# The last three pairs of a normalised matrix transposed by DMA in a fused graph layer on one Trainium2 core

## The reference, cut to what matters

```python
h = jnp.maximum(_layernorm(x, axis=-1), 0.0)            # "h0" below
type_sum = adj @ h                                      # the aggregate
attn_a = sigmoid(concat([type_sum, h], 1) @ Wa.T + ba)  # attn_b the same with Wb, bb
hw = h @ W_sa                                           # "mv" below, once scaled
s_left, s_right = hw @ a_sa[0, :256], hw @ a_sa[0, 256:]
scores = s_left[:, None] + s_right[None, :]
e = where(adj != 0, exp(-leaky_relu(scores, 0.01)), 0)
x_a = (e / (sum(e, 1) + 1e-5)) @ hw
x_b = adj @ (h @ W_gcnb) + b_gcnb                       # computed as (adj @ h) @ W_gcnb
out = x + sigmoid(attn_a * x_a + attn_b * x_b)
```

## Time and profile before

| | us |
|---|---|
| median of 3 runs (lowest, highest) | 179.05 (178.74, 179.24) |
| the profiled execution | 178.25 |
| its span in the trace | 176.4 |
| PE busy in the span | 171.6 |
| DVE busy | 147.0 |
| ACT busy | 115.4 |
| POOL busy | 18.6 |

### The profile page before, as it was taken

One profiled execution on the slowest core, in us unless ns is written; L12 is line 12 of the kernel. 1 busy time (PEld: TensorE's weight loads), 2 busy tenths in 40 slices (PEclk: granted clock), 3 DMA queues, 4 the chain that ended last, 5 costly groups with the idle time before them and its releaser, 6 DMA issues.

```text
span 176.4 us, 3397 instructions
## 1 busy us (share of the span) xinstructions
PE 171.6 (97%) x1324; PEld 125.8 (71%) x1324; DVE 147.0 (83%) x309; ACT 115.4 (65%) x169; POOL 18.6 (11%) x42
## 2 busy tenths in 40 slices
PE   7999999999999999999999999999999999999992
PEld 2556776654444468888844488888888888888892
DVE  3799997648999999799999922999999999976551
ACT  3679899642899988748494640675875884863310
POOL 4745436030000200000000000000000000000000
PEclk9999999999999999999999999999999999999999
DMA  5999996999991598000001100000010010011101
GB/s 129 288 260 260 224 181 116 202 206 211 298 423 43 82 214 180 0 4 2 0 4 59 59 0 4 0 0 0 4 59 0 6 59 0 4 61 59 60 33 30
DMA packets 5520, 16.87 MB, mean 96 GB/s; under 512 B 625, under 2 KB 1409, under 8 KB 4737
## 3 DMA queue, kind: packets, MB, share of 16 engines
q0 software_dynamic: 1584, 8.39, 24.6%
q1 hardware_dynamic: 3920, 8.27, 13.2%
HBM read 22.94 MB, written 2.11 MB: 142 GB/s over the span
## 4 chain that ended last, share of the span: by engine, by line
PE 94%; DMA 3%; DVE 1%; SPq 1%; issue 0%; ACT 0%; DVEq 0%
PE ps L773 31%; PE ps L815 16%; PE ps L816 16%; PE ps L814 16%; PE ps L751 6%; PE ps L807 6%; DMA wa_sb<-in_w_wide 3%; PE ps L745 2%; SPq L234 1%; PE ps L877 0%; DVE wa_hi L507 0%; DVE logit L724 0%; DVE e_lo L526 0%; ACT logit L411 0%; DVE res L631 0%
## 5 line engine op out<-in xcount | busy, mean ns | idle before, releaser
L814 PE MATMUL ps<-mv_lo,e_hi 128*128 128x257 f16 (+2 forms) x272 | 71.0, 267 | 0.0
L816 PE MATMUL ps<-mv_hi,e_lo 128*128 128x257 f16 (+2 forms) x272 | 70.8, 266 | 0.0
L815 PE MATMUL ps<-mv_hi,e_hi 128*128 128x257 f16 (+2 forms) x272 | 70.8, 266 | 0.0
L377 ACT ACTIVATE z<-z,log_e 128x1024 f32<-128x1024 f32 x32 | 36.7, 1146 | 29.1 <-DVE z L568 29.1
L568 DVE SCALAR_TENSOR_TENSOR z<-sl_row,exs,far 128x512 f32<-128x512 f32 x64 | 45.0, 743 | 0.0
L576 DVE TENSOR_TENSOR e_lo<-z,e_hi 128x1024 f16<-128x1024 f32 x32 | 38.9, 1216 | 1.2 <-ACT e_hi L387 1.2
L773 PE MATMUL ps<-adj,nat_lo 128*128 128x512 f16 x128 | 36.8, 379 | 0.0
L773 PE MATMUL ps<-adj,nat_hi 128*128 128x512 f16 x128 | 36.7, 379 | 0.0
L387 ACT ACTIVATE e_hi<-z 128x1024 f16<-128x1024 f32 x32 | 33.3, 1041 | 0.0
L815 PEld LDWEIGHTS ps<-mv_hi,e_hi 128*128 128x128 f16 x272 | 26.5, 98 | 3.2
L814 PEld LDWEIGHTS ps<-mv_lo,e_hi 128*128 128x128 f16 x272 | 26.4, 97 | 3.3
(11 more groups left out here) (69 smaller groups left out, 164.8 us busy)
## 6 DMA issues: line engine op xcount, KB each, us to landing
adj<-in_adj_t POOLq DMA_DIRECT2D x6, 1024.0 KB, 10.4
x_sb<-in_x SPq DMA_DIRECT2D x6, 512.0 KB, 8.9
out<-res SPq DMA_DIRECT2D x7, 256.0 KB, 2.0
adj<-in_adj_t POOLq DMA_DIRECT2D x3, 512.0 KB, 7.5
x_sb<-in_x SPq DMA_DIRECT2D x3, 256.0 KB, 4.8
sl_row<-sl_line SPq DMA_DIRECT2D x1, 768.0 KB, 9.7
adj<-in_adj_t POOLq DMA_DIRECT2D x2, 256.0 KB, 5.9
wa_sb<-in_w_wide SPq DMA_DIRECT2D x1, 258.0 KB, 4.5
```

Source lines behind the costliest of these rows:

```text
L377: act.activation(z[:, n % ZRING, :, :], z[:, n % ZRING, :, :], ACT.Exp, bias=log_e[:, 0:1], scale=SLOPE - 1.0).then_inc(exp_done, 1)
L814: pe.matmul(ps[:, bank, cols], e_hi[:, s, i1], mv_lo[:, j, cols], start=(j == 0), stop=False)
L815: pe.matmul(ps[:, bank, cols], e_hi[:, s, i1], mv_hi[:, j, cols], start=False, stop=False)
L816: return pe.matmul(ps[:, bank, cols], e_lo[:, s, i1], mv_hi[:, j, cols], start=False, stop=(j == NT - 1))
```

## The change

- PE transposes only units 0 to 5 (tiles 0 to 9, `NTURN` = 6). For pairs 5, 6 and 7 SP issues six DMA transposes (`turn_by_dma`), `nat_hi` and `nat_lo` of a pair each, straight into `h0t_hi` and `h0t_lo`; the layout of these becomes tile by tile. ACT and DVE no longer copy these three units out of PSUM.
- The wide products of pairs 5, 6, 7 (`wide(6)` to `wide(8)`) stand within the aggregate of chunk 1, after its tiles 7, 11 and 15. What follows from them on ACT (`mv_highs`) and DVE (`narrow_results`, `mv_lows`) stands in the loop over n, at n = 2 to 7.
- The row of s_left is in two halves of 8 tiles. `sl_lines(0)` stands at `wide(5)`, one unit later; `sl_lines(1)` after four tiles of the aggregate of chunk 2, on ACT at n = 8. `sl_spread(0)` stands on SP behind four of the six transposes, and now covers chunks 0 and 1.
- POOL asks for adj piece 5 one unit earlier, and waits for all six transposes before piece 7. SP asks for x again only when piece 7 has landed; the additions of 0.5 to it move from n = 2, 3, 4, 6 to 8, 9, 11, 12.

```diff
-SL_PARTS = ((0, 4), (4, 16))
-SL_UNIT = 4
+SL_PARTS = ((0, 8), (8, 16))
+SL_UNIT = 5
+LATE = 3
+ONTIME = NPAIR - LATE
+NTURN = NU - LATE
+WIDE_BANKS = (6, 2, 6, 2, 6, 2, 0, 2)
...
+            def turn_by_dma(p):
+                ts = slice(2 * p, 2 * p + 2)
+                for have, nat, h0t in ((nat_high, nat_hi, h0t_hi), (nat_ready, nat_lo, h0t_lo)):
+                    sp.wait_ge(have, p + 1)
+                    sp.dma_start(h0t[:, ts, :, :].rearrange("p t k n -> p (t k) n"),
+                                 nat[:, ts, :].rearrange("p t d -> p (t d)"),
+                                 transpose=True).then_inc(h0t_landed[p - ONTIME], 16)
+
+            sp.wait_ge(adj_landed[piece_of(0, NT - 1)], 16)
+            turn_by_dma(ONTIME)
             sl_store(0)
+            turn_by_dma(ONTIME + 1)
             sl_spread(0)
-            sl_store(1)
-            sp.wait_ge(turned, NU)
+            for p in range(ONTIME + 2, NPAIR):
+                turn_by_dma(p)
+            sp.wait_ge(adj_landed[piece_of(2, 0)], 16)
+            sp.wait_ge(turned, NTURN)
...
+            sl_store(1)
             sl_spread(1)
...
+            for p in range(ONTIME, NPAIR):
+                pool.wait_ge(h0t_landed[p - ONTIME], 32)
             load_adj(7)
...
-                    dve.wait_ge(sl_ready[min(c, 1)], 16)
+                    dve.wait_ge(sl_ready[c // 2], 16)
...
+                if n == 2:
+                    narrow_results(5)
+                if n == 3:
+                    mv_lows(5)
+                if n == 4:
+                    narrow_results(6)
+                if n == 5:
+                    mv_lows(6)
+                if n == 6:
+                    narrow_results(7)
                 if n == 7:
+                    mv_lows(7)
+                if n == 8:
                     agg_lows(1)
...
-            b_products(1, 0, 4)
-            pe.wait_ge(h0t_ready, NU)
+            b_products(1, 0, 8)
+            wide(6)
+            b_products(1, 8, 12)
+            pe.wait_ge(h0t_ready, NTURN)
+            wide(7)
+            b_products(1, 12, 16)
+            wide(8)
+            b_products(2, 0, 4)
             sl_lines(1)
-            b_products(1, 4, 16)
-            b_products(2, 0, 16)
+            b_products(2, 4, 16)
```

More of the change, by code:

```diff
@@ L136, in build @@
         part_b = sb("part_b", [P, 2, D], F32)
-        sl_turn = [part_b[0:hi - lo, h, 0:P] for h, (lo, hi) in enumerate(SL_PARTS)]
+        sl_turn = [c_sb[0:hi - lo, C_WT + h * P:C_WT + (h + 1) * P] for h, (lo, hi) in enumerate(SL_PARTS)]
         gated_b = sb("gated_b", [P, 2, 2, D], F32)
@@ L172, in build @@
         h0t_ready = sem("h0t_ready")
+        h0t_landed = [sem(f"h0t_landed{p}") for p in range(ONTIME, NPAIR)]
         wide_product = sem("wide_product")
@@ L310, in _ @@
             norms(5)
+            load_adj(5)
             norms(6)
-            load_adj(5)
             norms(7)
@@ L344, in h0t_highs @@
                 act.wait_ge(turned, u + 1)
-                act.activation(h0t_cols(h0t_hi, u), turn_bank(u), ACT.Copy).then_inc(h0t_high, 1)
+                act.activation(h0t_tiles(h0t_hi, u), turn_bank(u), ACT.Copy).then_inc(h0t_high, 1)
             def nat_highs(p):
@@ L431, in _ @@
                     nat_highs(p + 2)
-                mv_highs(p)
-            act.activation(factor_l[:, :], exs[:, :, SL], ACT.Exp, scale=SLOPE).then_inc(factors_done, 1)
+                if p < ONTIME - 1:
+                    mv_highs(p)
+            mv_highs(ONTIME - 1)
             agg_highs(0)
-            sl_lines(1)
             act.wait_ge(wg_landed, 16)
@@ L442, in _ @@
                     act_high(n - 1)
-                if n in (2, 3, 4):
-                    half_added(n - 2)
+                if n == 2:
+                    mv_highs(5)
+                if n == 4:
+                    mv_highs(6)
                 if n == 6:
+                    mv_highs(7)
+                    act.activation(factor_l[:, :], exs[:, :, SL], ACT.Exp, scale=SLOPE).then_inc(factors_done, 1)
+                if n == 7:
                     agg_highs(1)
-                    half_added(3)
+                if n == 8:
+                    sl_lines(1)
+                if n in (8, 9, 11, 12):
+                    half_added((8, 9, 11, 12).index(n))
                 if n == 10:
@@ L566, in dve_z @@
                 dve.wait_ge(far_ready, n + 1)
+                if ONTIME <= n < NPAIR:
+                    dve.wait_ge(exs_ready, n + 1)
                 for u in range(2):
@@ L651, in _ @@
             mv_lows(0)
-            for p in range(1, NPAIR):
-                if p + 1 < NPAIR:
-                    nat_lows(p + 1)
+            for p in range(1, ONTIME - 1):
+                nat_lows(p + 1)
                 if p > 1:
                     mv_lows(p - 1)
-                if p + 4 < NU:
-                    moments(p + 4)
+                moments(p + 4)
                 narrow_results(p)
-                if p + 1 < NPAIR:
-                    h0t_lows(p + 2)
-            mv_lows(NPAIR - 1)
+                h0t_lows(p + 2)
+            moments(NU - 1)
+            nat_lows(ONTIME)
+            mv_lows(ONTIME - 2)
+            narrow_results(ONTIME - 1)
+            for p in range(ONTIME + 1, NPAIR):
+                nat_lows(p)
+            mv_lows(ONTIME - 1)
             agg_lows(0)
@@ L755, in wide @@
             def wide(u):
-                pe.wait_ge(h0t_ready, u + 1)
+                if u < NTURN:
+                    pe.wait_ge(h0t_ready, u + 1)
+                else:
+                    pe.wait_ge(h0t_landed[u - NTURN], 32)
                 if u == 1:
```

34 lines of the change are left out of this document (18 added, 16 removed).

## The result

| | median, us | of runs | profiled execution | span | granted clock in it |
|---|---|---|---|---|---|
| before | 179.15 | 6 (178.43 to 179.63) | 178.25 | 176.4 | 1.00 |
| changed | 189.18 | 6 (186.22 to 192.42) | 186.22 | 184.4 | 0.991 |

The changed kernel is slower. The forecast was 183.2.

A forecast was written before the change was run, and what follows sets the result against it. PE, busy 97% of the span, was taken to bound the kernel. A 5.5 us wait for exs (57.8 against 52.3) less 1.3 dropped gave +4.2 on 179.05: 183.2 us, range 181 to 185.5, for 8 in 10 179.6 to 191.

The forecast's parts named there:

- What PE drops: PE's chain loses three units of transposes at 0.44 us each, a gain of 1.32 us if no wait is added.
- When PE comes to the waits: PE reaches the late wide products at 37.9, 42.7 and 47.5 us, chunk 2 at 48.85, `sl_lines(1)` at 52.3.
- The DVE loop: DVE's steps n = 0 to 6, from the first z to the last pair's exs, take 19.8 us without idle time.
- s: Start of z in DVE's step n = 0, which needs `sl_row`; taken as 38.0 us, bounds 35.2 to 44.0.
- s, by the row of s_left: Step timing DVE's first z by copy, store and spread of the row: spread landing at 37.9, z at 38.0 us.
- 28.4 + 4.7 = 33.1: ACT's copy of transposed s_left at 28.4 us, then 4.7 from store to spread issue, so spread issued at 33.1.
- I take 4.8: Time for the 512 KB spread to land, taken from 256 KB in the loaded opening; bounds 2.0 and 10.8 us.
- The sum by the median: Net +4.2 us (wait 5.5 less gain 1.3) put on the 179.05 us median, giving 183.2.
- I take 0, by the column: Extra cost of slower PE matmuls after the 5.5 us gap, taken as 0 from the granted clock; bounds 0 and 2.5.
- The second rival: PE's gap halves the clock, adding 2.5 us to the forecast's wait: 185.7 us, chance 0.18.
- Slow transposes: DMA transposes on SP land late, delaying adj piece 7 and the spread: 186 us and up, chance 0.16.
- the first rival: Slow transposes at 10.8 us a pair: PE waits 15.5 us, net +14, 193 us; chance 0.16 for 186 and up.

The follow-up runs named there:

- c2: e2 with the first half of the s_left row copied and stored earlier, its spread behind one transposed pair, adj piece 7 held for it: 177.89 us, ratio 0.993.
- e4: Changed kernel with 13 extra matmuls on PE ahead of `wide(8)` and 13 ahead of the second narrow transpose: 186.72 us, ratio 1.049.
- e1: Changed kernel with the first spread of the s_left row issued ahead of the second pair's transposes: 186.98 us, ratio 1.044.
- e6: Changed kernel with adj piece 6 asked for only when the store of the s_left line has landed: 187.92 us, ratio 1.052.
- c3: c2 with adj piece 6 asked for sooner, behind `norms(6)`: 178.22 us, ratio 0.991.
- e2: Changed kernel with the second narrow transpose (`sl_lines(1)`) eight tiles later on PE, its ACT copy at n = 6: 183.92 us.
- e5: e3 with adj pieces 7 and 8 held on POOL until the first spread has landed: 185.59 us, ratio 1.034.
- e3: Changed kernel without DMA transposes: PE turns all nine units, POOL asks for adj pieces 6, 7 and 8 in a row: 190.81 us, ratio 1.069.

## Why the forecast was right in sign and too small

**What PE drops: right as far as shown.** Twelve PE instructions less, and c2's median is 1.26 us below before's, forecast 1.32; its profiled execution is no quicker (above, under c2).

**When PE comes to the waits: right.** Forecast 48.85 behind `wide(8)` and 52.3 for the narrow transpose. In c2 PE starts `wide(8)` at 48.87, 1.1 us of it the wait at 17: 47.75, forecast 47.5. The narrow transpose stands eight tiles (6.9 us) later there, at 60.57; less these and the wait it is 52.5.

**The DVE loop: right.** From s to exs ready: 61.5 - 41.9 = 19.6, forecast 19.8. The wait of `wide(8)` was foreseen at s + 10 and measured at 51.94 - 41.88 = 10.1. That DVE has no idle time in the loop overlooks 0.30 us at 47.66; the changed kernel has the same, so it did no harm.

**s, by the row of s_left: this step failed.** Forecast "28.4 + 4.7 = 33.1", then "I take 4.8", s = 38.0. Measured 41.9, within the bounds given (35.2 to 44.0) but 3.9 off the value taken. The step took one store and one other DMA of before as the durations of its own:
- Store issued at 29.6 and not 28.4: +1.2. By e4 (no wait at 17 us, store at 28.57), e1 (0.90, 29.15) and the changed kernel (1.24, 29.61), it follows PE's wait for the adj piece; without that wait 28.4 holds. (The terms named make 24.8 + 1.4 + 1.7 = 27.9 for nat_hi where the text has 28.1, too little to matter.)
- Store 5.9 and not 4.7: +1.2. The 4.7 was itself a store beside adj. Without an adj piece asked for just before it, and with transposes ahead, it is 2.4 (e6); with piece 6 and no transposes ahead at most 3.1 (c2), but 8.0 beside pieces 5 and 6 (c3); with piece 6 and transposes ahead 5.9 to 6.6 (changed kernel, e1, e4) and once 12.1 (e2).
- Spread 6.3 and not 4.8: +1.5. The step said that the spread "shares the queues for 1 us only". For adj that holds (piece 6 landed at 35.7, 0.2 us into it), but it left out the third pair's transposes of its own change, which were on the way for all of it. With neither it took 4.3 (e5), with adj 9.4 (e3) and 10.3 (e6). That the transposes make the 1.5 is argued and not shown: with them and without adj it took 3.9, 4.4 and 5.0 in e2, c3 and e4, and 6.0 in e1.

The sum closes: s late by 3.9, the loop shorter by 0.2, makes +3.7, and the profiled execution came out at 186.22 where its sum said 182.45, +3.8.

**The sum by the median: also short.** The forecast put the same +4.2 on the median. But before lay 0.8 from its profiled execution to the median and the changed kernel 3.0. The path now runs over DMA landings, and these vary: the changed kernel's runs lie 6.2 us apart, before's 1.2, and c2's, where PE waits for nothing of the row, 1.8. So 3.8 of the missing 6.0 us is s in one execution, and 2.2 that this execution was the quickest of six. Whether later landings or the lower clock made the other five longer is open: only the quickest has a trace.

**The clock: "I take 0, by the column".** Wrong as a reading: the earlier trace rows reads 1.00 for an idle engine, and so did 48 to 52 us here, just before 0.50. In the opening of before the column reads 1.00 even beside the matmuls that are 0.44 us apart, so there it is no witness at all:

```profile
1.20:2.50 1.30, 1.30 (x4) 0.47 (x5) 0.00 (x0) 1.00 (x2) 0.28 (x1) 1.00 0.47 121
```

The second rival, that the gap halves the clock, thus came true, but its 2.5 us didn't: 1.7 us, and nothing of the sum in the profiled execution (e4). The forecast cites the Trainium skill, "TensorE: Matmul & The Clock Gate", section "Why this matters for your kernels", by which the clock falls back to half after an idle gap. The traces agree in part: 0.50 behind the 2.94 us here, 2.75 in e1 and 4.51 in e2, 0.58 behind 2.14 in e6, but 1.00 behind the 2.99 us here and 3.61 in e5. What else decides no run here shows.

**Slow transposes: partly.** Per transpose 5.3 to 6.1 us to landing in the median, by the rows of the page's list of DMAs (count, us):

```profile
e_hi<-nat_hi SPq DMA_TRANSPOSE x3, 6.1
e_lo<-nat_lo SPq DMA_TRANSPOSE x3, 5.3
```

The last landed at 42.9 and not by 41; piece 7, asked for then, landed at 50.9 and fell inside the wait of `wide(8)`. No row shows the 10.8 a pair of the first rival in this execution; in e2 single transposes took up to 14.6 us, and PE waited 2.06 for one. Of the two estimates named there the first is near for one DMA: 1309 ns a block by the Trainium skill, "VectorE: DVE Perf Modes", the three transpose paths, where one DMA of four blocks landed after 4.6 to 6.4 us, 1.2 to 1.6 a block. They overlap, so its estimate of 31 us for all six is too long; the estimate of 2 us by the rate of a regular DMA in the Trainium skill, "Advanced Engine Details and Errata", X-Bar Transpose (TRN2), is too short for even one. From the first issue to the last landing 17.7 us passed (25.2 to 42.9), with waits for `nat_lo`, the store and the spread in between.

**Not decided.** Whether the wait at 17 us is the change's; how much of the median's 2.5 us between the changed kernel and e4 is clock; how much of the 1.5 us on the spread is the transposes'; what held all DMAs in e2.

## What to carry to other kernels

When a change lets PE wait for a chain that starts with a small DMA, price that DMA by what runs beside it, with its own change's transfers on the list, and give it a range: the same 512 KB took 3.9 to 6.3 us here without adj beside it and up to 10.3 with, and a 4 KB store 1.2 to 12.1. Before moving work off the critical engine, list every stop at which it will meet the late chain, not only the last: mending one (e2) shows the next, and the median fell below before's, by 1.26 us, only when all had slack (c2). And look at several executions once the path leads over a DMA, as one profile may be the quickest.

## What the runs showed of the hardware

- A DMA transpose of 128 x 512 f16 (128 KB) held SP for 1.2 to 1.4 us at its issue and took 4.6 to 6.4 us to land in the changed kernel; over all runs the issue took 1.2 to 3.2 us, once 6.00 (e2), and the landing 2.3 (e6) to 14.6 (e2). It moves in small packets: under 512 B there were 625 in the kernel before, and after:

```profile
DMA packets 8783, 17.66 MB, mean 96 GB/s; under 512 B 3888, under 2 KB 4672, under 8 KB 8000
```

- Holding back 2 MB of adj (pieces 7 and 8) on POOL's queue made a 512 KB DMA of SP's queue 5.1 us quicker (e3 to e5).
- In e2 a 4 KB store, a 1 MB piece of adj and a transpose took 12.1 to 14.6 us, and for 3 us of these the DMA engines moved 8 GB/s.
- An idle time of PE of 2.94 us was followed by 0.50 of the clock in the matmuls behind it; one of 1.24 us, in the opening, and one of 2.99 us before `sl_lines(1)`, by none, nor was one of 3.61 us in e5.
- In the first microseconds of the trace the granted clock reads 1.00 beside matmuls of 512 columns 0.44 us apart.
